# A vision-tower kernel on one core: the order of TensorE, ScalarE and VectorE work inside each slot of the head

## What is computed

```python
h = layer_norm(x @ fc0_w + fc0_b)                  # 32 channels per point
for i in range(4):
    x1 = spectral_conv(h, w1[i], w2[i])            # Fourier modes 12 x 12, mixed over channels
    x2 = einsum('bchw,oc->bohw', h, conv_w[i]) + conv_b[i]   # the channel mix
    h = layer_norm(x1 + x2)                        # times ln_g, plus ln_b
    if i < 3: h = gelu(h)
h = gelu(h @ fc1_w + fc1_b)                        # the head: 32 -> 128
h = gelu(h @ fc2_w + fc2_b)                        # 128 -> 64
h = (h @ fc3_w + fc3_b)[..., 0]                    # 64 -> 1
h = h + attention(layernorm(h))                    # then a small attention stage
h = h + experts(layernorm(h))                      # and a feed-forward with 8 experts
```

## Time and profile before

| what | value |
|---|---|
| median of 3 runs | 5455.23 us (5449.39 to 5459.40) |
| the profiled execution | 5451.53 us |
| its span, first to last instruction | 5449.8 us |
| TensorE busy | 4984.3 us, 91% |
| VectorE, ScalarE busy | 3838.4 us (70%), 3866.9 us (71%) |
| GpSimd busy | 891.3 us, 16% |
| the head pass, from the first fc1 to the last | 3145.4 to 4715.0 us |
| granted TensorE clock, mean of the span | 0.969 |

### The profile page before, as it was taken

How to read it: one execution, slowest core, us unless ns; L and a number is a source line. 1 busy time by engine, 2 the same in 40 slices (tenths; PEclk the granted TensorE clock), 3 DMA queues, 4 the chain that set the end, 5 groups by cost and what they waited for, 6 DMA issues and landing times.

```text
span 5449.8 us, 134904 instructions
## 1 busy us (share of the span) xinstructions
PE 4984.3 (91%) x43556; PEld 2874.9 (53%) x43556; DVE 3838.4 (70%) x7702; ACT 3866.9 (71%) x6261; POOL 891.3 (16%) x1359
## 2 busy tenths in 40 slices
PE   5888899999999999999999999999999999768777
PEld 2444567666767666776667734433333333334433
DVE  4888899888989888998888955555455554354454
ACT  5999877888767888777887766677777777523333
POOL 0134221333212332222332200000000000000000
PEclk9999999999999999999999999999999999878888
DMA  1344567677777676776677722311111111000000
GB/s 63 136 144 165 158 204 242 230 236 231 241 236 238 225 241 226 250 247 229 224 241 238 243 82 69 70 47 55 48 51 54 47 54 47 11 4 4 8 8 4
DMA packets 222595, 756.33 MB, mean 139 GB/s; under 512 B 74033, under 2 KB 113202, under 8 KB 156730
## 3 DMA queue, kind: packets, MB, share of 16 engines
q1 hardware_dynamic: 175162, 632.45, 33.9%
q0 software_dynamic: 47104, 119.60, 8.9%
HBM read 397.49 MB, written 354.42 MB: 138 GB/s over the span
## 4 chain that ended last, share of the span: by engine, by line
PE 59%; DVE 13%; ACT 12%; issue 11%; DMA 2%; SPq 1%; ACTq 1%; DVEq 1%; POOL 0%; POOLq 0%
PE ps_y L924 9%; PE ps_t L1030 8%; PE ps_t L936 5%; PE ps_y L916 5%; PE ps_f L924 4%; PE ps_f L1015 4%; PE ps_t L945 4%; ACT big L1174 3%; PE ps_t L1039 2%; PE ps_s L961 2%; ACT big L1183 2%; PE ps_y L1000 2%; DVE big L1358 2%; DVE big L1339 2%; ACT big L1178 2%
## 5 line engine op out<-in xcount | busy, mean ns | idle before, releaser
L1358 DVE TENSOR_REDUCE big<-big 128x16 f32<-128x512 f32 x1280 | 857.0, 680 | 677.2 <-ACT big L1174 674.4
L1351 DVE TENSOR_TENSOR big<-big 128x512 f32<-128x512 f32 x1280 | 886.7, 699 | 32.9 <-DVE big L1380 18.6
L1174 ACT ACTIVATE big<-ps_y 128x512 f32<-128x512 f32 x892 | 550.2, 617 | 470.1 <-PE ps_y L924 417.6
L1190 ACT ACTIVATE big<-ps_t,g_now 128x512 f32<-128x512 f32 x1024 | 823.5, 804 | 7.9 <-PE ps_t L936 7.9
L936 PE MATMUL ps_t<-ident,big 128*128 128x128 f32 x5120 | 793.1, 278 | 30.3 <-DVE big L1351 22.4
L924 PEld LDWEIGHTS ps_y<-conv_now,big 128*128 128x128 f32 x5088 | 617.2, 191 | 362.8 <-issue 362.8
L1183 ACT ACTIVATE big<-ps_t 128x512 f32<-128x512 f32 x1024 | 635.3, 620 | 158.5 <-PE ps_s L961 111.4
L924 PE MATMUL ps_y<-conv_now,big 128*128 128x128 f32 x5088 | 717.9, 284 | 0.0
L936 PEld LDWEIGHTS ps_t<-ident,big 128*128 128x128 f32 x5120 | 572.2, 141 | 275.5 <-issue 233.8
L945 PE MATMUL ps_t<-ident,big 128*128 128x128 f32 x4096 | 634.8, 278 | 70.3 <-ACT big L1183 65.0
L945 PEld LDWEIGHTS ps_t<-ident,big 128*128 128x128 f32 x4096 | 466.0, 142 | 227.5 <-issue 117.1
(11 more groups left out here) (197 smaller groups left out, 7619.5 us busy)
## 6 DMA issues: line engine op xcount, KB each, us to landing
hstore<-big SPq DMA_DIRECT2D x256, 1024.0 KB, 4.2
big<-hstore SPq DMA_DIRECT2D x256, 1024.0 KB, 5.3
xmodes<-x_out SPq DMA_DIRECT2D x128, 312.0 KB, 4.4
y_kt<-ymodes SPq DMA_DIRECT2D x512, 78.0 KB
ymodes<-y_st POOLq DMA_DIRECT2D x192, 144.0 KB, 5.7
ymodes<-y_st POOLq DMA_DIRECT2D x64, 192.0 KB, 5.4
mix_room<-xmodes POOLq DMA_DIRECT2D x32, 336.0 KB, 7.3
mix_room<-xmodes POOLq DMA_DIRECT2D x64, 168.0 KB, 9.0
```

The lines of the kernel that those rows point to most:

```text
L1174: af(y_sq[wh], of[:, wh, :], ACT.Square).then_inc(s["sq_done"], 1)
L1190: af(h_new[k // 2][:, at:at + 512], ps_t1[:, :], ACT.Identity if kind == "stem" else ACT.Gelu, bias=g_now[:, 1:2], scale=g_now[:, 0:1]).th ...
L1351: v_.tensor_tensor(groups(y_sb[2 * k + wh]), groups(y_sb[2 * k + wh]), rstd[:, k // 2, at:at + 16].unsqueeze(2).to_broadcast([128, 16, 32] ...
L1358: v_.tensor_reduce(ss[:, k // 2, at:at + 16], groups(y_sq[wh]), AX.X, ALU.add).then_inc(s["ss_done"], 1)
```

## The change

All of it lies in the slot of the head pass.

- TensorE: `inv_h` goes up, in front of mix and `inv_w`. The first turn of a slot (`turn_out(turned - 1, ..)`) goes from before them to behind them, right in front of the first conv. `fc3` goes from before the first conv to behind the next fc2. The second turn goes from before `fc2(v, 1)` to behind it, right in front of the second conv.
- ScalarE: `square` of the second half goes in front of the slot's last `g2`.
- VectorE: mix and `turn_z` go in front of `take_xt` and `normed` of the second half. `take_tok` goes behind `rsqrt_half`.

No instruction is added or taken away, and the lists of SyncE and GpSimd are as before.

```diff
@@ -1123,7 +1123,8 @@
                 fc1(v, 0, iw_count, mixed)
                 if not opening:
                     fc2(v - 1, 1)
-                    turn_out(turned - 1, "head", k, 1, pair - 1)
+                if front is not None:
+                    inv_h(n, k, False)
                 if visit is not None:
                     mix(*visit, ps_f, 2 * v + 1)
                 if (k == 0 and front in MIXED) or (k == 2 and nxt in MIXED):
@@ -1132,17 +1133,17 @@
                         inv_w(n, 1, 0, 0, ps_f)
                     else:
                         inv_w(n + 1, 0, 0, 0, ps_f)
-                if front is not None:
-                    inv_h(n, k, False)
                 if not opening:
-                    fc3(pair - 1, 2 * pair + 2)
+                    turn_out(turned - 1, "head", k, 1, pair - 1)
                 if front is not None:
                     conv(k, 0, False)
                 fc2(v, 0)
+                if not opening:
+                    fc3(pair - 1, 2 * pair + 2)
                 fc1(v + 1, 1, iw_later, mixed if visit is None else mixed + visit[5])
+                fc2(v, 1)
                 if kind is not None:
                     turn_out(turned, kind, (k + 1) % 4, 0, pair)
-                fc2(v, 1)
                 if front is not None:
                     conv(k, 1, False)
                 fc2(v + 1, 0)
@@ -1251,9 +1252,10 @@
                         g1(v + 1, 0)
                         g2(v, pair, 0, 1)
                         g1(v + 1, 1)
+                        if front is not None:
+                            square(unit + 1, 1, ps_y)
                         g2(v + 1, pair, 1, 0)
                         if front is not None:
-                            square(unit + 1, 1, ps_y)
                             keep_y(unit + 1, k, 1, ps_y)
                         continue
                     if front in MIXED and back1 in STORED:
@@ -1467,11 +1469,6 @@
                     turn_w(n - 2, 1, ps_f)
                 if k == 1 and back2 in STORED:
                     turn_modes(n - 2)
-                if not opening:
-                    take_xt(turned - 1, 1)
-                    if fresh is not None or k == 2:
-                        late = 2 * (4 * n + k - 3)
-                        normed(late + 1, 2 * n - 2 + (k + 1) // 2, (k + 1) % 4, 1)
                 if visit is not None:
                     mix(*visit, ps_f)
                 if k == 0 and front in MIXED:
@@ -1479,11 +1476,15 @@
                 if k == 2 and nxt in MIXED:
                     turn_z(n + 1, 0, ps_f)
                 if not opening:
-                    take_tok(pair - 1, (k - 1) % 4, n - 1 if k else n - 2)
+                    take_xt(turned - 1, 1)
+                    if fresh is not None or k == 2:
+                        late = 2 * (4 * n + k - 3)
+                        normed(late + 1, 2 * n - 2 + (k + 1) // 2, (k + 1) % 4, 1)
                     if k == 0:
                         rsqrt_half(n - 1, 1)
                     if k == 2 and front is not None:
                         rsqrt_half(n, 0)
+                    take_tok(pair - 1, (k - 1) % 4, n - 1 if k else n - 2)
                 if front is not None:
                     sums(unit, k, 0)
                 if kind is not None:
```

## The result

| | before | after |
|---|---|---|
| median of 4 runs each | 5452.57 us (5449.39 to 5459.40) | 5373.89 us (5371.60 to 5378.73) |
| the profiled execution | 5451.53 us | 5371.60 us |
| its span | 5449.8 us | 5369.9 us |
| head pass, first fc1 to last | 3145.36 to 4714.99: 1569.6 us | 3143.95 to 4634.93: 1491.0 us |

After over before is 0.9858, with a 95% interval of 0.9843 to 0.9873. The change makes the kernel faster by 79 us, 1.4%, and the interval is well clear of 1. 5382 had been predicted, with a range of 5372 to 5404. The two traces put nearly all of the gain into the head pass: 78.7 us. The passes ahead of it differ by 1.4 us and what follows by 0.1.

A forecast was written before the change was run, and what follows sets the result against it. TensorE, busy 1146.4 of 1160 us in the head loop, was taken as the bound. Terms of 46.9 + 16.6 + 2.4 + 3.1 + 1 - 3 + 4 = 71 us gave 5382 us, range 5372 to 5404.

The forecast's parts named there:

- The pair: Head pass: a turn right in front of a conv saves 0.19 us, 247 times, 46.9 us in all.
- Rival 2: Head pass: turn and conv do not pair, so 46.9 us are not gained, 5429 us; chance 6%.
- Inverse h as cover: Head slots with inverse w or mix: inverse h ahead covers the wait for g1, gaining 16.6, 2.4 and 3.1 us.
- The handshake through fc3: Head slots: g2 waits for fc3, and fc2 for g2; no stall taken, up to 18 us possible.
- Rival 1: Head slots: fc2's wait for g2, and g2's for fc3, binds, and take_tok too; 5396 us; chance 12%.
- rival 3: Head slots: g2 releases fc2 0.74 us later than worked out, price exceeds gain; 5493 us, slower; chance 2%.
- `take_tok`: Head slots 0 and 2: standing behind rsqrt, it stalls the second turn about 0.06 us, 46 times in the loop: -3 us.
- The last body: End of the head pass, no conv: 7 or 8 waits of about 0.85 us become 0.3 us, 4 us gained.
- The first two slots: Start of the head pass: the first slot's wait shrinks by the inverse h swap, about 1 us gained.

## Why the prediction was right, and which terms were off

**The pair (46.9 us predicted).** Odd loop slots, which hold two pairs and no other edit's effect, went from 11.54 to 11.15: 0.391 us, or 0.195 a pair. For 247 pairs that is 48.2 us. The rows of a layer's pass gave the price of the head's pairs to 0.005 us, by their starts and by the load that begins early. Rival 2, no pairing in the head, is refuted by the load at 3875.48 and by the two runs that break one pair each. It takes the whole shape: before the change conv stood behind fc3 and fc2, which have its 128 rows but 32 and 64 columns, and a turn behind fc1, with 128 columns but 32 rows, and none of these gained anything (1.09 and 0.59 us).

The rule weighed there, from the Trainium skill's "TensorE: Matmul & The Clock Gate", section on row and column tiling, is that loads overlap with matmuls in flight only when the row group differs. The trace does not agree: turn and conv both use all 128 rows, and the load at 3875.48 runs beside the transposition. The same section also says that a load into the background weight buffer is pulled ahead whatever its rows; a load that begins early would fit that, but no run here shows which buffer it goes to. The page "TensorEngine Tiling (Array Packing)", section Key Properties, says that a change of the tiling mode drains the engine, and with 0.09 us for leaving a shape the trace agrees in kind.

**Inverse h as cover (16.6 + 2.4 + 3.1 us).** Of the loop's even slots 0.739 - 0.391 = 0.348 us are this term, net of `take_tok`: 16.0 us in 46 of them. The unrolled slots and the quad behind the loop gained 17.3 us, of which 30 slots x 0.391 = 11.7 are pairs, so 5.6 are waits. Together 21.6 net of `take_tok`, against 22.1 worked out without it. The inverse h run alone shows 12.80 to 12.44, the full 0.36.

**The handshake through fc3 (no stall; up to 18 us allowed for).** ScalarE and TensorE of after, in order of time:

```profile
3855.57 0.69 ACT L1203 ACTIVATE big<-ps_t,fc_b 128x512 f32<-128x512 f32 x1 [0.93 <-PE ps_t L1039]
```

```profile
3854.37 1.06 PE L1039 MATMUL ps_t<-big,fc_w 128*32 128x512 f32 x8
...
3856.44 1.08 PE L1030 MATMUL ps_t<-big,fc_w 128*64 128x512 f32 x4
```

`g2` starts 1.20 us after fc3, which is the value that was taken. It ends at 3856.26, and fc2 starts at 3856.44, in its turn: 0.18 us of slack, predicted 0.17. ScalarE's wait of 0.93 us for fc3 is new, and it costs nothing. Rival 1 did not come about. What rival 3 feared is seen only in the run with fc3 behind fc1.

**`take_tok` (-3 us).** The mechanism was right and its size too large. VectorE and TensorE of after, even slot:

```profile
3865.34 0.65 DVE L1402 COPY w_raw<-ps_t 128x512 f32<-128x512 f32 x1
3865.91 0.67 DVE L1353 TENSOR_TENSOR big<-big 128x512 f32<-128x512 f32 x1
3866.50 0.18 DVE L1366 TENSOR_SCALAR big<-big 128x64 f32<-128x64 f32 x1
...
3868.65 0.74 DVE L1413 TENSOR_SCALAR big<-ps_t,fc_b 128x512 f32<-128x512 f32 x1
```

```profile
3868.49 1.08 PE L1030 MATMUL ps_t<-big,fc_w 128*64 128x512 f32 x4
3869.54 0.63 PE L936 MATMUL ps_t<-ident,big 128*128 128x128 f32 x4
```

From start to start `take_xt` and `normed` take 0.57 and 0.59 us, not 0.60 and 0.65. `take_tok` ends at 3869.39. The turn starts 1.05 us after fc2, where 1.01 is the time without a wait, and the conv behind it comes sooner, so that a slot loses about 0.01 us: 0.5 us in all. The slack is as thin as that. The run with the first turn early moved TensorE ahead by some 0.4 us there, and lost 0.39 in every even slot. Its expectation, one pair and nothing else, had missed that.

**The last body (4 us).** It gave 4.1. The idle time of the earlier trace rows is now 0.25 us instead of 0.83:

```profile
4604.83 1.08 PE L1030 MATMUL ps_t<-big,fc_w 128*64 128x512 f32 x4 [0.25 <-issue]
```

**The first two slots (1 us predicted, and 0.6 of pairs).** This is the term that was mis-sized: 5.3 us. The prediction counted a single wait there, and left out both VectorE's chain and the clock. The busy times of slot 0 and slot 1, with the granted clock behind POOL's, first of before, then of after:

```profile
3145.36:3160.97 15.61, 14.34 (x76) 5.57 (x76) 3.23 (x4) 7.38 (x10) 0.00 (x0) 0.71 0.08 24
3160.97:3177.76 16.79, 15.68 (x128) 6.80 (x120) 7.77 (x12) 8.22 (x11) 0.84 (x2) 0.90 0.01 1
```

```profile
3143.95:3157.07 13.12, 13.12 (x76) 4.74 (x77) 3.91 (x5) 7.78 (x11) 0.00 (x0) 0.79 0.10 31
3157.07:3171.06 13.99, 13.74 (x129) 6.12 (x121) 7.18 (x12) 8.20 (x11) 0.83 (x2) 1.00 0.01 2
```

TensorE in order of time in slot 1, before and after, shows the wait of fc1's second half for VectorE's `turn_modes`, and what an fc2 takes at half clock (1.76 us instead of 1.08):

```profile
3163.21 1.13 PE L1021 MATMUL ps_s<-w_raw,fc_w 32*128 32x512 f32 x4 [1.11 <-DVE fw_sb L1345]
3164.27 1.76 PE L1030 MATMUL ps_t<-big,fc_w 128*64 128x512 f32 x4
```

```profile
3158.44 1.13 PE L1021 MATMUL ps_s<-w_raw,fc_w 32*128 32x512 f32 x4 [0.25 <-DVE fw_sb L1347]
```

By an estimate from these rows, the waits shrink by 1.27 us in slot 0 (idle 15.61 - 14.34, now none; that is the term of 1 us) and by 1.11 - 0.25 = 0.86 in slot 1. The share of the time at half clock costs TensorE half of its speed: in slot 1 16.79 x 0.10 = 1.7 us, and now nothing; in slot 0 15.61 x 0.29 = 4.5, less some 0.6 in which it waited anyway, against 13.12 x 0.21 = 2.8, so 1.1. With 0.6 for three pairs that is 5.5, against 5.3 seen. The early `square` is behind the 0.86 (it lets VectorE's sums and `turn_modes` come earlier), as the run with the square late shows, where the 1.11 is back and slot 1 has a clock of 0.90 again. In all nine traces with the early square this wait is 0.24 or 0.25 us, and in the three without it 1.11.

```profile
3156.47:3172.91 16.44, 15.33 (x128) 6.31 (x121) 7.61 (x12) 8.19 (x11) 0.84 (x2) 0.90 0.01 1
```

That a wait of 1.11 us brings the clock down is not shown. The run with inverse h alone had the same wait in slot 1 and a clock of 1.00 there (slot 1 took 15.10 us). Slot 0 took from 12.37 to 13.32 us in the nine traces in which TensorE has no idle time in it, with a mean clock of 0.78 to 0.85, after's 13.12 among them. What stays open is how much of the 2.8 us of clock belongs to the change and how much to chance.

**The sum.** 47.7 us of pairs behind the first two slots (244 of them), 21.6 of waits net of `take_tok`, 5.3 in the first two slots and 4.1 in the last body make 78.7, against 71. Of the 7.7 us between them 3.7 are the first slots (5.3 less 1 and less 0.6 for pairs), 2.5 `take_tok`, 1.3 the pairs (48.2 against 46.9), and the rest is rounding.

## What to carry to other kernels

On an engine that is never idle, look for what a group of instructions costs by its neighbours: two groups of 128 x 128 side by side saved 0.195 us against the same groups apart, two of 128 x 32 saved 0.14, and the price can be read from any place in the trace where they already stand so. Before you move a group past others, write down when each result is due and when its bank comes free. Here the good order has slacks of 0.18 us at fc3's handshake and none at `take_tok`; one place further, fc3 cost 1 us a slot, and moving one turn ahead of inverse h cost 0.39 in slots with rsqrt besides its pair. Where a wait can't be shortened, put ahead of the waiting group one that doesn't need the same bank.

## What the runs showed of the hardware

- A weight load starts 0.11 us ahead of its first matmul, beside the last matmul of the group before it, if the tile shape is the same, even though both use all rows. That was seen for 128 x 128 and for 128 x 32 (mix and fc3 in the run with inverse h up). Of the 0.195 us that this is worth at 128 x 128, 0.09 is saved at the end of the first group and 0.10 at the start of the second; at 128 x 32 it is 0.11 and 0.03. Four groups in a row save 0.15 more than two pairs.
- The granted clock in the first two slots differs between variants with the same work there (0.79 and 0.85 in slot 0), and twice it was below full level in slot 1 behind a wait of 1.11 us, once not. Where slot 0 has no idle time, its length still differs by up to 0.95 us.
- TensorE's two halves of fc1 come interleaved, 0.01 us apart. Where the copy that they read ends 0.35 us ahead of them and not 1.00, the second half starts 0.13 us behind the first, and the row names no idle time. A turn that starts 0.13 us late for `take_tok` has no idle time in its row either. Such stalls are seen only in the starts.
